# Expert blocks of a graph layer: gated rows turned by VectorE alone, tokens gathered two blocks ahead

## The reference

```python
x = x + gnn(xn, src, dst, ...) + mix(xn)
x = x + moe(layernorm(x))

def moe(flat):                                   # E, K = 8, 2; D, H = 512, 1024
    logits = flat @ router_w.T
    topk_vals, topk_idx = top_k(logits, K)
    topk_w = softmax(topk_vals)
    g = einsum('sd,edh->esh', flat, w_gate)
    u = einsum('sd,edh->esh', flat, w_up)
    y = einsum('esh,ehd->esd', silu(g) * u, w_down)
    return einsum('esd,se->sd', y, dense_w)      # dense_w: topk_w at topk_idx
```

## Time and profile before

| | before |
|---|---|
| three runs | 1516.67, 1519.42, 1522.49 us; median 1519.42 us |
| the profiled execution | 1516.8 us, of which its span is 1515.1 us |
| PE / DVE / ACT / POOL busy over the span | 90% / 66% / 41% / 49% |
| the experts' stage | from 1045.6 us (first product) to 1515.1 us |
| PE busy from 1101 to 1464 us (17 blocks) | 362.8 of 363.0 us |
| DVE busy in the same stretch | 202.1 us |

### The profile page before, as it was taken

The page is one execution under the profiler, slowest core; times in us unless marked ns, Lnnn a source line. Parts: engine busy times, 40 slices in busy tenths (PEclk is TensorE's granted clock), DMA queues, the critical chain, the costliest instruction groups (busy, mean ns, idle before and its releaser), DMA issues.

```text
span 1515.1 us, 24461 instructions
## 1 busy us (share of the span) xinstructions
PE 1363.7 (90%) x6696; PEld 641.6 (42%) x6697; DVE 995.6 (66%) x2508; ACT 627.5 (41%) x1094; POOL 735.2 (49%) x763
## 2 busy tenths in 40 slices
PE   6656998868869999999999999885799999999997
PEld 4343444435534444444444444472333333433333
DVE  7946666567837777777777777775445565556554
ACT  4455555645525666666666666571011101111110
POOL 3777777777766555555556555205212112211121
PEclk8788999989979999999999999996999999999999
DMA  5665333333248888888878888572243551524513
GB/s 192 221 210 174 115 117 117 114 112 112 100 158 283 249 249 249 249 248 249 248 237 258 248 249 248 178 279 65 60 131 91 185 189 28 194 58 150 194 28 94
DMA packets 125875, 262.51 MB, mean 173 GB/s; under 512 B 21073, under 2 KB 64808, under 8 KB 125147
## 3 DMA queue, kind: packets, MB, share of 16 engines
q0 software_dynamic: 48416, 141.37, 31.3%
q1 hardware_dynamic: 77410, 120.57, 23.7%
HBM read 204.35 MB, written 63.66 MB: 177 GB/s over the span
## 4 chain that ended last, share of the span: by engine, by line
PE 61%; POOL 21%; issue 7%; DMA 5%; DVE 4%; SPq 2%; ACT 0%; POOLq 0%; DVEq 0%; ACTq 0%
POOL edge_list L446 20%; PE psum L1325 19%; PE psum L1813 16%; PE psum L1825 8%; PE psum L1338 7%; PE psum L1333 5%; PE psum L1320 2%; DMA xrow<-in_x 1%; SPq L1722 1%; DMA out_sums<-xrow 1%; SPq L369 1%; DMA out_x<-out_sums 1%; PE psum L1820 1%; DVE shared L1407 1%; PE psum L1516 0%
## 5 line engine op out<-in xcount | busy, mean ns | idle before, releaser
L1216 POOL DMA_INDIRECT shared<-node_table,shared x328 | 310.2, 946 | 213.1 <-DVE msg L1293 126.7
L446 POOL DMA_INDIRECT edge_list<-rec,place x313 | 312.7, 999 | 98.7 <-issue 94.8
L1295 DVE TENSOR_TENSOR msg<-shared,psum 128x768 f32<-128x768 f32 x328 | 311.1, 949 | 0.0
L1325 PE MATMUL psum<-wf,hT 128*128 128x512 f32 x656 | 305.6, 608 | 3.5 <-ACT psum L1250 2.8
L1813 PE MATMUL psum<-shared,zT 128*64 128x512 f32 (+1 forms) x960 | 295.7, 597 | 1.7 <-DVE zT L1931 1.5
L1250 ACT COPY psum<-bias 128x512 f32<-128x512 f32 x328 | 193.2, 590 | 212.2 <-DVE msg L1295 195.0
L1293 DVE TENSOR_TENSOR msg<-shared,psum 128x256 f32<-128x256 f32 x328 | 136.5, 416 | 138.9 <-PE psum L1325 120.9
L1813 PEld LDWEIGHTS psum<-shared,zT 128*64 128x64 f32 (+1 forms) x960 | 114.3, 159 | 180.8 <-issue 178.7
L1325 PEld LDWEIGHTS psum<-wf,hT 128*128 128x128 f32 x656 | 118.3, 190 | 156.0 <-issue 137.5
L1825 PE MATMUL psum<-shared,hidT 128*64 128x512 f32 (+1 forms) x480 | 154.8, 601 | 7.7 <-DVE hidT L1952 7.7
L1774 POOL DMA_DIRECT2D ids<-slot_list x20 | 11.7, 583 | 297.3 <-DVE zN L1900 267.8
(11 more groups left out here) (338 smaller groups left out, 1513.8 us busy)
## 6 DMA issues: line engine op xcount, KB each, us to landing
shared<-edge_list SPq DMA_DIRECT2D x332, 130.0 KB
shared<-in_L_ffn_w_gate SPq DMA_DIRECT2D x8, 2048.0 KB, 9.1
shared<-in_L_ffn_w_up SPq DMA_DIRECT2D x8, 2048.0 KB, 14.8
shared<-in_L_ffn_w_down SPq DMA_DIRECT2D x8, 2048.0 KB, 19.5
shared<-node_table,shared POOLq DMA_INDIRECT x328
edge_list<-rec,place POOLq DMA_INDIRECT x313, 2.6
raw<-in_records SPq DMA_DIRECT2D x19, 256.0 KB, 3.6
xrow<-in_x SPq DMA_DIRECT2D x10, 250.0 KB
```

What stands on the lines that cost most here:

```text
L446: nc.gpsimd.indirect_dma_start(out=edge_list, out_offset=bass.IndirectOffsetOnAxis(ap=place[:n_, c:c + 1].bitcast(U32), axis=0), in_=rec[: ...
L1216: nc.gpsimd.indirect_dma_start(out=gat[:, k % G, :], out_offset=None, in_=table, in_offset=bass.IndirectOffsetOnAxis(ap=ix, axis=0)).then_ ...
L1295: nc.vector.tensor_tensor(m[:, 1:7, :].rearrange("p (a i) f -> p a i f", a=2), g[:, P:D].rearrange("p (i f) -> p i f", i=3).unsqueeze(1).t ...
L1325: nc.tensor.matmul(WP[k % TS][:], hT[:, (k // TS) % 2, (k % TS) * P:(k % TS + 1) * P], wf2[:], start=False, stop=True, skip_group_check=Tr ...
```

## The change

- VectorE turns both halves of the gated rows. TensorE's `turn_hidden`, ScalarE's copy into `hidT` and their semaphores go.
- The second up product is split into two pieces of 256 columns, in banks 3 and 5 (`PIECES`). VectorE multiplies and turns each piece by itself: 16 transposes of 32x64 each, in place of none. One semaphore (`hid_turned`) counts three arrivals for each block, and TensorE waits for them before m = 0, 4 and 6 (`READY`).
- VectorE turns the next block's tokens at the start of a block, ahead of the products' results, no longer at its end.
- Tokens are gathered two blocks ahead: the first three blocks' node numbers come from one-hot products (a third `picks`, `first_tokens`, `read_ids`), and the list is two blocks longer.
- GpSimd's loop is in another order: scatter first, then the next node numbers, then (once the scatter has landed) the targets of the next finished block, then the gather. The first targets are loaded ahead of the wait for `acc_in`, and the last ones need no buffer of their own.

```diff
@@ banks and pieces
-                GATE, UP, Y, TURNED = (bank[0], bank[2]), (bank[1], bank[3]), bank[4], (bank[7], bank[5])
+                GATE, UP, Y = (bank[0], bank[2]), ((bank[1],), (bank[3], bank[5])), bank[4]
+                PIECES = ([(0, D)], [(0, D // 2), (D // 2, D)])
+                READY = {0: 1, HM // 2: 2, HM // 2 + HM // 4: 3}
@@ GpSimd
                     gather(first_ids[:, 1:2])
-                    enter(6, 2 * NC_)
+                    enter(6, 10)
+                    pool.wait_ge(ids_found, 3)
+                    pool.wait_ge(turned, 3)
+                    gather(first_ids[:, 2:3])
+                    enter(10, 2 * NC_)
                     pool.wait_ge(y_out, LISTED)
+                    pool.dma_start(to[:], slot_list[0:BLK, :]).then_inc(to_in, 16)
+                    pool.wait_ge(to_in, 16)
                     pool.wait_ge(acc_in, 16 * NC_)
-                    with pool.Fori(2, nb + 1) as b:
-
-                        wait_alone(pool, turned, b + 1)
-                        pool.dma_start(ids[:], slot_list[bass.ds(b * BLK, BLK), :]).then_inc(ids_in, 16)
-                        wait_alone(pool, y_out, b * 16 + (LISTED - 32))
-                        pool.dma_start(to[:], slot_list[bass.ds(b * BLK - 2 * BLK, BLK), :]).then_inc(to_in, 16)
-                        wait_alone(pool, ids_in, b * 16 - 16)
+                    with pool.Fori(1, nb) as b:
+
+                        give(b + 1)
+                        wait_alone(pool, turned, b + 3)
+                        pool.dma_start(ids[:], slot_list[bass.ds(b * BLK + 2 * BLK, BLK), :]).then_inc(ids_in, 16)
+                        wait_alone(pool, y_out, b * 16 + LISTED)
+                        pool.dma_start(to[:], slot_list[bass.ds(b * BLK, BLK), :]).then_inc(to_in, 16)
+                        wait_alone(pool, ids_in, b * 16)
                         gather(ids[:, 0:1])
-                        wait_alone(pool, to_in, b * 16 - 16)
-                        give(b)
-                    pool.dma_start(last_to[:], slot_list[bass.ds(nb * BLK - BLK, BLK), :]).then_inc(to_in, 16)
-                    wait_alone(pool, to_in, nb * 16)
-                    wait_alone(pool, y_out, nb * 16 + (LISTED - 16))
+                        wait_alone(pool, to_in, b * 16 + 16)
@@ TensorE
-                            hidden(GATE[0], wgate, 0)
-                            hidden(UP[0], wup, 0)
-                            hidden(GATE[1], wgate, 1)
-                            hidden(UP[1], wup, 1)
-                            pe.wait_ge(first_turned, b + 1)
+                            for h_ in range(2):
+                                hidden(GATE[h_], wgate, h_, 0, D)
+                                for q_, (c0, c1) in enumerate(PIECES[h_]):
+                                    hidden(UP[h_][q_], wup, h_, c0, c1)
                             pe.wait_ge(y_bank, b + 1)
-                            for m in range(HM // 2 - 1):
-                                down(m)
-                            turn_hidden(1)
-                            down(HM // 2 - 1)
-                            pe.wait_ge(hid_copied, b + 1)
-                            for m in range(HM // 2, HM):
+                            for m in range(HM):
+                                if m in READY:
+                                    pe.wait_ge(hid_turned, b * len(READY) + READY[m])
                                 down(m)
...
+                    first_tokens(2)
@@ ScalarE
-                        act.wait_ge(hid_turned, b + 1)
-                        nc.scalar.copy(hidT[:, DJ:HM, :], TURNED[1][:].rearrange("p (q n) -> p q n", q=DJ)).then_inc(hid_copied, 1)
@@ VectorE
                         dve.wait_ge(zt_done, b + 1)
+                        turn(b * 16 + 32)
+                        if last is None:
+                            read_ids(2)
                         for h_ in range(2):
                             dve.wait_ge(silu_done, b * 2 + (h_ + 1))
-                            dve.wait_ge(gu_mm, b * 4 + (2 * h_ + 2))
-                            ins = nc.vector.tensor_tensor(hid[:, h_, :], sg[:, h_, :], UP[h_][:], ALU.mult)
-                            if h_ == 0:
-                                ins.then_inc(hid_first, 1)
-                                dve.wait_ge(hid_first, b + 1)
+                            for q_, (c0, c1) in enumerate(PIECES[h_]):
+                                dve.wait_ge(gu_mm, b * 5 + (2 * h_ + q_ + 2))
+                                nc.vector.tensor_tensor(hid[:, h_, c0:c1], sg[:, h_, c0:c1], UP[h_][q_][:, 0:c1 - c0], ALU.mult).then_inc(hid_done, 1)
+                                dve.wait_ge(hid_done, b * len(READY) + (h_ + q_ + 1))
+                                m0, m1 = h_ * DJ + c0 // P, h_ * DJ + c1 // P
                                 for i in range(BLK // W):
                                     for q in range(P // W):
-                                        ins = nc.vector.transpose(hidT[q * W:(q + 1) * W, 0:DJ, i * W:(i + 1) * W],
-                                                                  hid[i * W:(i + 1) * W, 0, :].rearrange("t (j p) -> t j p", j=DJ)[:, :, q * W:(q + 1) * W])
-                                ins.then_inc(first_turned, 1)
-                            else:
-                                ins.then_inc(hid_done, 1)
-                        turn(b * 16 + 32)
+                                        ins = nc.vector.transpose(hidT[q * W:(q + 1) * W, m0:m1, i * W:(i + 1) * W],
+                                                                  hid[i * W:(i + 1) * W, h_, c0:c1].rearrange("t (j p) -> t j p", j=m1 - m0)[:, :, q * W:(q + 1) * W])
+                                ins.then_inc(hid_turned, 1)
                         copy_turned(b + 3)
```

More of the change, by code:

```diff
@@ L154, in gps_layer @@
         z_rows = nc.dram_tensor("z_rows", (N + P, D), F32, kind="Internal").ap()
-        slot_list = nc.dram_tensor("slot_list", ((NBLK + 1) * BLK, 2), F32, kind="Internal").ap()
+        slot_list = nc.dram_tensor("slot_list", ((NBLK + 3) * BLK, 2), F32, kind="Internal").ap()
         acc = nc.dram_tensor("out_sums", (N + P, D), F32, kind="Internal").ap()
@@ L1698, in gps_layer @@
             yraw = sbi("yraw", [P, D])
-            sums_in, last_to = sbi("sums_in", [P, D]), sbi("last_to", [P, 2])
+            sums_in = sbi("sums_in", [P, D])
             last_in, last_out = sem("last_sums_loaded"), sem("last_rows_out")
-            ids_in, z_in, turned, zt_done, gu_mm, silu_done, hid_done, hid_turned, hid_copied, y_mm, y_bank, y_out = (sem(n_) for n_ in (
-                "ids_loaded", "tokens_gathered", "tokens_turned", "tokens_copied", "gate_up_mm", "silu_done", "hidden_done", "hidden_turned_b", "hidden_copied_b",
+            ids_in, z_in, turned, zt_done, gu_mm, silu_done, hid_done, hid_turned, y_mm, y_bank, y_out = (sem(n_) for n_ in (
+                "ids_loaded", "tokens_gathered", "tokens_turned", "tokens_copied", "gate_up_mm", "silu_done", "hidden_done", "hidden_turned_b",
                 "down_mm", "down_bank", "down_added"))
             LISTED = 16 * 2 * NC_
-            gated, hid_first, first_turned = sem("gated"), sem("hidden_first"), sem("hidden_first_turned")
+            gated = sem("gated")
             picked_s, ids_mm, ids_found, to_in, stored = (sem(n_) for n_ in (
@@ L1808, in run_blocks, with hidden @@
                         with pe.Fori(first, end) as b:
-                            def hidden(dest, w, h_):
+                            def hidden(dest, w, h_, lo_c, hi_c):
                                 for j in range(DJ):
                                     for lo, hi, u in parts:
-                                        ins = nc.tensor.matmul(dest[lo:hi, :], zT[:, j, lo:hi], w[u][:, j, h_ * D:(h_ + 1) * D],
+                                        ins = nc.tensor.matmul(dest[lo:hi, 0:hi_c - lo_c], zT[:, j, lo:hi], w[u][:, j, h_ * D + lo_c:h_ * D + hi_c],
                                                                start=(j == 0), stop=(j == DJ - 1), skip_group_check=True)
                                 ins.then_inc(gu_mm, 1)
-                            def turn_hidden(h_):
-                                pe.wait_ge(hid_done, b + 1)
-                                for q in range(DJ):
-                                    ins = nc.tensor.transpose(TURNED[h_][:, q * BLK:(q + 1) * BLK], hid[:, h_, q * P:(q + 1) * P], ident)
-                                ins.then_inc(hid_turned, 1)
                             def down(m):
@@ L1928, in _ @@
                     picks(1)
+                    link(nc.vector.tensor_scalar(slot_f[:CR], slot_f[:CR], -float(BLK), 0.0, ALU.add, ALU.max))
+                    in_block(2)
                     read_ids(1)
+                    picks(2)
                     dve.wait_ge(turned, 2)
@@ L1964, in _ @@
                     dve.wait_ge(y_mm, nb)
```

(2 more changed lines are left out.)

22 lines of the change are left out of this document (11 added, 11 removed).

## The result

The changed kernel takes 1578.97 us (median of 4 runs, 1577.19 to 1580.69), the kernel before on the same chip 1519.98 us (4 runs): a ratio of 1.0385, with a 95% interval of 1.0367 to 1.0402. It is 59 us slower; 51 were forecast. The profiled execution took 1578.63 us with a span of 1576.9.

The account below looks back on a forecast made before the run. TensorE bound the kernel before, and VectorE's chain would after: 38.9 us in steady blocks, 0.8 at the beginning, 1.7 at the end and 9.5 for the clock made +50.9 us, 1570 us as a median, range 1531 to 1592.

Parts of the forecast that it names:

- What bounds it, and the sign: Steady blocks: TensorE bounds before, VectorE's chain after; slower, chance 0.85.
- The price of a small transpose: VectorE's 32x64 transposes: 236 ns each, 0.249 us from start to start, 3.98 us for 16.
- proportional: Rival on VectorE's transposes: price goes by size, 0.158 us each, no wait left, -10 us, 1509 us; chance 0.12.
- all fixed: Rival on VectorE's transposes: whole price fixed, 0.316 us each, blocks of 25.7 us, +78 us, 1603 us or more; chance 0.04.
- The 36 ns: VectorE's transposes: the fixed part said to be left if price were proportional to size, held against that rival.
- the copy's 147 ns: VectorE's 64x64 copy: its fixed part, called near 170 and far from 36, the reason for taking 0.249 us.
- the range's upper end, 1592: Whole kernel: top of the range from 1531 us, said to be where the clock falls at each wait.
- The steady block: Blocks 2 to 19: 23.55 us against 21.39, with TensorE waiting 2.7 us before m = 6; +38.9 us over 18 blocks.
- The clock: TensorE's granted clock: falls behind one new wait in three, costing 1.5 us each, +9.5 us; bounds none and 28.5.
- The beginning: Blocks 0 and 1: the targets' stall goes, the tokens' turn takes its place, block 2 starts at 1101.5 us; +0.8 us.
- The third one-hot product: The beginning: the added product for the third block's node numbers is hidden under the first gather.
- The end: Last block: TensorE ends at 23.55 us, the sums' copy goes at about 14, last scatter starts at about 25.2; +1.7 us.

Follow-up runs that it names:

- the repeat: The changed kernel run once more, not a line different: one execution, 1575.86 us, beside 1517.07 us for the kernel before.
- the wait filled: The changed kernel with two matmuls of 512 columns that nobody reads in TensorE's wait before m = 6: 1572.65 us, ratio 1.0356.
- two waits in a block: The kernel before with only VectorE's turn of the second half in two pieces, tokens' turn still last: 1668.57 us, ratio 1.0995.
- two waits of 0.9 to 1.0 us: The changed kernel with the second half cut into 384 and 128 columns, not 256 and 256: 1563.25 us, ratio 1.0295.
- early targets: The kernel before with targets loaded early: 1516.96 us, ratio 0.9997; a second form, its wait for the last load moved earlier: 1516.16 us, ratio 0.9997.

## Why the prediction was right, step by step

**What bounds it, and the sign: right.** VectorE took TensorE's place as the bound. Leaving half of the new transposes out turned the loss into a gain of 0.25%, and giving the turn back to TensorE took 53 of the 59 us away.

**The price of a small transpose: right.** 236 ns and 3.98 us for 16, as forecast; this decided against the rivals (proportional, 0.158 us from start to start; all fixed, 0.316 us). A small transpose, too, starts only when the last is over: (3.98 - 0.236)/15 = 0.250 us from start to start. This agrees with the rule that the prediction cites from the Trainium skill, page "VectorE: DVE Perf Modes", section "Two Vector instructions with no wait between them": an instruction whose output starts in another group of 32 partitions is held until the earlier ones have finished. By the 151 cycles of that page's section on the errata, given there for a tensor_tensor, a small transpose would be 224 ns as an estimate, and the trace has 236. Over 18 blocks of 32 transposes that is 7 us less in the sum (the prediction says 6), farther from what came. Two details of the working don't hold. The 36 ns that it leaves as the fixed part of the proportional case don't follow from its rows, since a price that goes by size leaves none; the copy's 147 ns spoke against that case all the same. And the range's upper end, 1592, stands 3 us above the 1589 that its own terms give with a fall at each wait.

**The steady block: right, a little small.** Forecast 23.55 us with a wait of 2.7 before m = 6; measured 23.76 and 2.5. VectorE's last piece came 0.07 us later, the rest is TensorE's start behind it and its last two products. Over 18 blocks 42.9 us instead of 38.9.

**The clock: the mechanism right, its size too large.** 9.5 us were set aside, for a fall behind one wait in three. Of the 50.4 us of the 18 blocks 42.9 are the usual block and 2.5 the gaps told next; about 5 remain, in five blocks with a clock of 0.93 to 0.99. These are three falls, two of which reach into the next block, so one in six waits and 1.5 to 1.7 us each. In the repeat there are five falls and some 8 us. The fall comes behind a wait of 2.48 us, and these rows show its price, m = 6 and 7 (four records) in 2.89 us where 1.98 is usual:

```profile
1349.37 2.89 PE L1824 MATMUL psum<-shared,hidT 128*128 128x512 f32 x4 [2.48 <-DVE hidT L1952]
1352.06 14.75 PE L1818 MATMUL psum<-shared,zT 128*128 128x512 f32 x40
```

The same wait of 2.48 us in front of 1542.92 was followed by no fall (m = 6 and 7 in 1.98 us, the 40 records of gate and up in 13.92). The length of the wait doesn't decide, and no view here tells which ones fall. With the wait filled there was no fall in these blocks.

**A term that the sum lacked: the change of expert.** Three times in the steady blocks TensorE idles, for up to 1.1 us, with nothing to wait for:

```profile
1324.42 1.94 PE L1824 MATMUL psum<-shared,hidT 128*64 128x512 f32 x8 [2.53 <-DVE hidT L1952]
1327.45 2.84 PE L1818 MATMUL psum<-shared,zT 128*128 128x512 f32 x6 [1.09 <-issue]
```

Here TensorE's program reads the block numbers of the next two experts, which it does at three of the seven changes of expert, and the gaps stand at these three and nowhere else. The kept trace has this work of the sequencer, which no view shows: at the first gap it begins at 1204.64 us, 0.24 us after the wait before m = 6 has ended, and the gate product comes at 1207.46. So it takes 2.8 us, and the two down products behind the wait cover only 1.7 of them. Before, it was done while more products were queued: the only such gap was 0.2 us. Three more runs agree: with one piece, so four products behind the wait, there is no such gap, nor is there one where half of the transposes are left out and TensorE doesn't wait; with pieces of 384 and 128, one product behind the wait, the gaps are 1.1 to 2.0 us. It is 2.5 us in all.

**The beginning: two errors, 3.0 us instead of 0.8.** The third one-hot product was costed at nothing, hidden under the first gather. But it stands behind that gather and the first turn of tokens, and the sequencer reads the first block numbers only behind it:

```profile
1049.89 0.71 PE L1804 MATMUL psum<-tok_b,pick 125*128 125x1 bf16 x20
1052.67 3.78 PE L1818 MATMUL psum<-shared,zT 128*128 128x512 f32 x4 [2.07 <-issue]
```

The reading begins 9.65 us after the routing's last step where it was 8.64, and the first gate product starts 12.3 us after that step, not 11.2: 1.1 us, and as much with TensorE's turn. And the first targets were forecast at 1079.5 us; they came 47.2 us after the routing, 3.2 earlier than before, not 5:

```profile
1087.51 0.49 DVE L1934 TENSOR_SCALAR yo<-yraw,to 128x512 f32<-128x512 f32 x1 [9.90 <-DMA to<-slot_list]
...
1098.81 8.26 PE L1824 MATMUL psum<-shared,hidT 128*128 128x512 f32 x12 [4.17 <-DVE hidT L1952]
```

The step itself is right: from the weighting to m = 0 it is 11.30 us, as summed (11.3). The stall on the targets shrank and the tokens' turn filled its place.

**The end: 2.5 us instead of 1.7.** The copy of the sums went out 15.0 us after the last block's start (forecast 14), and the last scatter stood behind it:

```profile
1559.71 0.63 SPq L1736 DMA_DIRECT2D out_x<-out_sums  x1
...
1568.67 0.75 DVE L1962 SCALAR_TENSOR_TENSOR yo<-psum,to,sums_in 128x512 f32<-128x512 f32 x1 [1.70 <-PE psum L1824]
1570.67 1.01 POOL L1793 DMA_INDIRECT out_x<-yo,to  x1 [13.64 <-DMA out_x<-out_sums]
```

It starts 25.9 us after the block, 0.7 later than forecast.

**In sum**, from the routing on: 42.9 (38.9) for the usual block, 5 to 8 (9.5) for the clock, 2.5 (0) at the experts, 3.0 (0.8) at the beginning, 2.5 (1.7) at the end: 56 to 59 us where 50.9 were forecast. The total is nearer than its terms, and some of that is luck: the clock's share came out 1.5 to 4.5 us too large, and the other four were 9.5 us too small together.

## What to carry to other kernels

Before work is moved to an engine with slack, lay out that engine's chain inside one block, from the product at which it starts to the product that waits for it: VectorE was 56% busy before, yet with 32 transposes more in a block its last result came 2.5 us too late each time. Splitting a piece to overlap it pays the fixed part again (here 170 ns of 236 for each transpose), and helped here only with the smaller piece last. And keep a wait that isn't over in time away from the end of a loop body: what stands behind it must also cover the sequencer's work between loops.

## What the runs showed of the hardware

- One wait of 2.5 us in each block of 24 us was followed by a fall of the granted clock three times in 18 blocks (five times in the repeat, six with a single piece). With two waits in a block, of 2.75 and 2.5 us on the mean, no block had the full clock. With two waits of 0.9 to 1.0 us it fell only behind the two idle times of 1.9 us and more at a change of expert, and with waits of 0.6 to 0.8 us it stayed at 1.00 from 1156 to 1520 us. A fall cost 1.5 to 1.8 us.
- A late wait costs more than its own length: TensorE's sequencer couldn't run ahead, and of its 2.8 us of register work between loops 0.3 to 1.1 us showed as idle time put down to "issue" with two products behind the wait, 1.1 to 2.0 us with one.
- Ahead of the blocks, one program's time scatters by 2 to 5 us between executions, so a difference of two profiles should be counted from a step behind that.
- A stream transpose of 32 partitions in float32 took 203, 236, 270 and 303 ns for 32, 64, 96 and 128 elements, and each waited for the last to end.
- With early targets the last scatter started 7.3 us earlier, counted from the routing, and landed as fast; but GpSimd's closing DRAIN took 6.77 us, not 3.14, in all three profiles. The cause is open.
